# A graph kernel's prologue: edge counts shifted on TensorE, node rows gathered for 125 nodes at once, the input table split on GpSimd

## The reference, cut to what matters

```python
edge_index = jnp.stack([src, dst])
x = _layernorm(x + _L0_gnn_ref(x, src, dst, L0_gnn_W, L0_gnn_b), axis=-1)
x = _layernorm(x + _L1_gnn_ref(x, edge_weight, src, dst), axis=-1)
x = _layernorm(x + _L2_gnn_ref(x, edge_weight1, src, dst, L2_gnn_W1, L2_gnn_b1, L2_gnn_W2, L2_gnn_b2), axis=-1)
x = _layernorm(x + _L3_gnn_ref(x, edge_index, L3_gnn_W1_l, L3_gnn_b1, L3_gnn_W1_r, L3_gnn_W2_l, L3_gnn_b2, L3_gnn_W2_r), axis=-1)

# in L0, and alike in the others:
sums = jax.ops.segment_sum(h[src], dst, num_segments=N)
deg = jax.ops.segment_sum(jnp.ones((src.shape[0],), h.dtype), dst, num_segments=N)
h_total = jnp.concatenate([h, sums / jnp.maximum(deg, 1.0)[:, None]], axis=1)
```

## Time and profile before

| What | Value |
|---|---|
| median of 3 executions | 4041.06 us (4039.64 to 4046.97) |
| the profiled execution's own time | 4037.8 us |
| its span in the trace | 4035.9 us |
| busy share of the span | PE 73%, PE weight load 70%, DVE 55%, ACT 23%, POOL 35% |
| start of the first build matmul | 343.85 us |

### The profile page before, as it was taken

How to read it: one execution, slowest core, us unless ns; L and a number is a source line. 1 busy time by engine, 2 the same in 40 slices (tenths; PEclk the granted TensorE clock), 3 DMA queues, 4 the chain that set the end, 5 groups by cost and what they waited for, 6 DMA issues and landing times.

```text
span 4035.9 us, 119777 instructions
## 1 busy us (share of the span) xinstructions
PE 2965.3 (73%) x52730; PEld 2823.6 (70%) x52730; DVE 2213.4 (55%) x3076; ACT 937.2 (23%) x1994; POOL 1393.3 (35%) x1262
## 2 busy tenths in 40 slices
PE   0636999999995888888984655655555556489898
PEld 0635999999994878888874544555545555489898
DVE  8955777677766554455656555555545555411122
ACT  0004777777771000000000111111111111100000
POOL 5478100000000000000007777777777777600100
PEclk9999999999995999999996777777777777799999
DMA  4414787777884999999974333343333333287797
GB/s 122 83 35 128 272 289 286 269 284 273 287 288 163 402 403 391 403 391 404 400 325 114 93 92 99 99 109 92 91 100 97 104 97 99 69 346 288 261 380 312
DMA packets 334176, 891.87 MB, mean 221 GB/s; under 512 B 124164, under 2 KB 199032, under 8 KB 304088
## 3 DMA queue, kind: packets, MB, share of 16 engines
q1 hardware_dynamic: 279400, 835.28, 55.9%
q0 software_dynamic: 44480, 47.34, 5.6%
q10 hardware_dynamic: 9792, 1.93, 0.3%
HBM read 634.20 MB, written 250.86 MB: 219 GB/s over the span
## 4 chain that ended last, share of the span: by engine, by line
PE 32%; POOL 28%; issue 16%; DMA 15%; DVE 5%; ACT 1%; SPq 1%; POOLq 1%; DVEq 1%; ACTq 0%
POOL stream L931 27%; DMA stream<-a_weights 13%; PE ps L1287 13%; PE ps L1333 6%; PE ps L1260 5%; PE ps L1328 5%; POOL stream L909 1%; DVE junk L1615 1%; DMA a_counts<-stream 1%; ACT stream L1041 1%; DVE junk L1693 1%; DVE stream L1678 1%; PE ps L1394 1%; PE ps L1228 1%; SPq L675 0%
## 5 line engine op out<-in xcount | busy, mean ns | idle before, releaser
L931 POOL DMA_INDIRECT stream<-table,stream x990 | 1091.0, 1102 | 1998.9 <-DMA stream<-dst_run 1697.3
L1287 PE MATMUL ps<-operand_room 64*128 64x50 bf16 (+1 forms) x18750 | 635.1, 221 | 17.3 <-DVE operand_room L1860 8.0
L1475 PE MATMUL ps<-edge_room,stream 125*128 125x64 bf16 x2970 | 196.2, 242 | 609.5 <-DVE stream L2227 581.3
L1287 PEld LDWEIGHTS ps<-operand_room 64*128 64x128 bf16 x18750 | 613.8, 163 | 42.5 <-DVE operand_room L1860 8.5
L1333 PE MATMUL ps<-stream,node_room 125*64 125x125 f32 x10000 | 565.0, 273 | 92.8 <-DMA stream<-a_weights 85.6
L1475 PEld LDWEIGHTS ps<-edge_room,stream 125*128 125x128 bf16 x2970 | 185.4, 162 | 619.4 <-DVE stream L2227 416.8
L1333 PEld LDWEIGHTS ps<-stream,node_room 125*64 125x64 f32 x10000 | 542.0, 137 | 108.1 <-DMA stream<-a_weights 98.3
L1041 ACT CAST stream<-ps 128x500 bf16<-128x500 f32 (+2 forms) x700 | 431.3, 633 | 194.3 <-PE ps L1287 155.1
L1041 ACT COPY stream<-ps 128x500 f32<-128x500 f32 (+2 forms) x700 | 422.1, 619 | 0.0
L1328 PE MATMUL ps<-operand_room,stream 125*125 125x192 bf16 x3750 | 326.8, 250 | 4.4 <-POOLq L567 4.4
L1328 PEld LDWEIGHTS ps<-operand_room,stream 125*125 125x125 bf16 x3750 | 321.8, 140 | 4.6 <-POOLq L567 4.6
(11 more groups left out here) (269 smaller groups left out, 3516.4 us busy)
## 6 DMA issues: line engine op xcount, KB each, us to landing
stream<-a_weights SPq DMA_DIRECT2D x100, 3125.0 KB, 16.7
a_weights<-stream SPq DMA_DIRECT2D x500, 312.5 KB
stream<-a_counts SPq DMA_DIRECT2D x100, 1562.5 KB, 9.1
a_counts<-stream SPq DMA_DIRECT2D x500, 156.2 KB
node_room<-sorted_edges SPq DMA_DIRECT2D x120, 352.0 KB
stream<-dst_run SPq DMA_DIRECT2D x30, 1056.0 KB, 5.8
stream<-table,stream POOLq DMA_INDIRECT x990
node_room<-sorted_edges SPq DMA_DIRECT2D x40, 256.0 KB
```

Source lines behind the costliest of these rows:

```text
L931: pool.indirect_dma_start(emsg[s][:, t, :], None, tables[L2][:, :], bass.IndirectOffsetOnAxis(src_t[j % 3][:, at:at + 1], 0))\
L1287: ins = pe.matmul(out if step == 0 else out[:, 1:2], low[s][rows_a, :, t], planes[s][rows_a, t // TI, what, :, t % TI], start=step == 0, s ...
L1475: ins = pe.matmul(ps_q[:, t * D:(t + 1) * D], hot_dst[0:Q, :, at], qparts[0:Q, POOL_BLOCKS[i], v * D:(v + 1) * D], start=v == 0, stop=v == 2)
```

## The change

- `upto` gets a column of zeros on its left (`upto_pad`), and the identity matrix gets zeros around it (`ident_pad`). Two matmuls on PE, placed behind histogram 12 and a wait for `upto`, give `below`: one shifts by a partition, the other moves the last partition of a column to the first of the next. The writes to memory and the reads back are gone.
- `node_at` holds one value for each of the 125 nodes of a column. POOL gathers 125 nodes with one indirect DMA (50 in all, none of which waits for the flag), into buffers of their own.
- The 15 transposes of a chunk of keys become 30 f32 matmuls with every second column of the identity: for even nodes into partitions 0 to 63 of PSUM, for odd nodes into 64 to 127.
- The spill's table is made at column 23 of the loop instead of 32, and its 50 matmuls lie between histograms 4 to 12, six behind each (the last two behind 12).
- On DVE the wait for `below` stands behind histogram 12; 21 histograms follow it. Before, 15 stood ahead of it and 6 behind.
- The split of x is done on POOL in ten pieces of five tiles behind the gathers and the flag; PE waits for all ten ahead of block 1.

```diff
+    KG = 2
+    KGATHERS = KCH // KG
+    SPILL_FROM, SPILL_STEP, COUNTED = 4, 6, 13
...
-            sp.wait_ge(upto_rdy, 1)
-            sp.dma_start(edges_upto[1:N_NODES + 1].rearrange("(j q) -> q j", q=Q), upto[0:Q, :],
-                         allow_slow_non_contiguous=True).then_inc(upto_out, 16)
...
-            sp.wait_ge(upto_out, 48)
-            sp.dma_start(below[0:Q, :], edges_upto[0:N_NODES].rearrange("(j q) -> q j", q=Q),
-                         allow_slow_non_contiguous=True).then_inc(below_in, 16)
-            for a in range(3):
-                evens = edges_upto[a:a + N_NODES].rearrange("(j q) -> q j", q=Q)[0:Q:2, :]
-                sp.dma_start(upto3[0:COLS, a, :], evens, allow_slow_non_contiguous=True).then_inc(below_in, 16)
...
+            def gather_nodes():
+
+                for j in range(NPP):
+                    at = j % KC * DEG * 3
+                    pool.indirect_dma_start(node_rows[j // KC][0:Q, at:at + DEG * 3], None, packed[:, :],
...
                 if mode == "linear":
-                    gather_nodes(KRING, KCH)
+                    for lo in range(0, NPP, KC):
+                        split(pool, pieces(L0, lo, lo + KC), xcur[0:Q, lo:lo + KC, :], total[0][0:Q], parts_rdy)
...
-            gather_nodes(0, KRING)
+            gather_nodes()
             both(pool, run)
...
                 ins.then_inc(hist_used, 1)
-
-            pe.wait_ge(spill_rdy, 1)
-            for j in range(NPP):
-                ins = pe.matmul(bank(3)[0:Q, j:j + 1], spill[:, j, :], last_w[:, :], start=True, stop=True)
-            ins.then_inc(wspill, 1)
+                if m == SPILL_FROM:
+                    pe.wait_ge(spill_rdy, 1)
+                if m >= SPILL_FROM:
+                    for j in range((m - SPILL_FROM) * SPILL_STEP, min((m - SPILL_FROM + 1) * SPILL_STEP, NPP)):
+                        pe.matmul(bank(3)[0:Q, j:j + 1], spill[:, j, :], last_w[:, :], start=True, stop=True)\
+                          .then_inc(wspill, 1)
+                if m == COUNTED - 1:
+                    pe.wait_ge(upto_rdy, 1)
+                    pe.matmul(ps_below, ident_pad[0:Q, 0:Q], upto[0:Q, :], start=True, stop=False)
+                    pe.matmul(ps_below, ident_pad[0:Q, Q:2 * Q], upto_pad[0:Q, 0:NPP],
+                              start=False, stop=True).then_inc(below_ps, 1)
...
                         for j in range(KC):
-                            ins = pe.transpose(ps_key[c % 2][v][:, j, :], rows_of[0:PITCH, j, :, v],
-                                               ident[0:PITCH, 0:PITCH])
+                            for a in range(2):
+                                ins = pe.matmul(ps_key[c % 2][v][a * DEG:(a + 1) * DEG, j, :],
+                                                rows_of[0:Q, j, :, v], ident[0:Q, a:P:2], start=True, stop=True)
...
                 for jj in range(JI):
+                    if jj == 1:
+                        pe.wait_ge(parts_rdy, KCH)
                     build_block(0, jj)
...
-                if j == 32:
+                if j == 23:
+                    v.memset(upto_pad[:, 0:1], 0.0)
                     fill_spill(1)
...
-            for m in range(13, 28):
-                histogram(m)
-
-            v.wait_ge(below_in, 64)
+            v.wait_ge(below_ps, 1)
+            v.tensor_copy(n(below), ps_below)
+            v.drain()
+            v.tensor_copy(n(node_at), n(below)).then_inc(node_rdy, 1)
             v.tensor_tensor(n(deg), n(upto), n(below), ALU.subtract)
...
-            for m in range(28, STEPS):
+            for m in range(COUNTED, STEPS):
                 histogram(m)
...
-                    for lo, hi in ((0, PART), (PART, NPP)):
-                        split(v, pieces(L0, lo, hi), xcur[0:Q, lo:hi, :], x_rest[0:Q, lo:hi, :], parts_rdy)
                     keys()
```

More of the change, by code:

```diff
@@ L189, in build_program @@
                   .rearrange("p (u i h t) -> p u i h t", i=4, u=TO, t=TI) for b in range(2)]
[L190 to L194, removed]
+        PART = NPP // 2
+        GOTW = KC * DEG * 3
+        node_rows = [in_room(stream, c * GOTW, GOTW) for c in range(KCH - 1)] + [in_room(node_room, 0, GOTW)]
+        far_tmp = in_room(stream, KCH * GOTW, KC * DEG).rearrange("p (j t) -> p j t", t=DEG)
+        key_tmp = [in_room(stream, KCH * GOTW + (i + 1) * KC * DEG, KC * PITCH) for i in range(2)]
+        assert KG * KGATHERS == KCH and PART % KC == 0 and KC == GT and (KCH - 1) * GOTW <= 4 * CH
+        assert SPILL_FROM + -(-NPP // SPILL_STEP) <= COUNTED and GOTW <= EPP
         pack_all = in_room(operand_room, 2320, 3 * EPP).rearrange("p (t v) -> p t v", v=3)
@@ L280, in build_program @@
         start_i = sb("start_i", [P, NPP], I32)
-        node_f, blk_f, cnt, upto, below, deg, has, dinv, norm, norm_has, tmpn, wend, wcarry = (
-            sb(n, [P, NPP]) for n in ("node_f", "blk_f", "cnt", "upto", "below", "deg", "has", "dinv", "norm",
+        node_f, blk_f, cnt, below, deg, has, dinv, norm, norm_has, tmpn, wend, wcarry = (
+            sb(n, [P, NPP]) for n in ("node_f", "blk_f", "cnt", "below", "deg", "has", "dinv", "norm",
                                       "norm_has", "tmpn", "wend", "wcarry"))
-        upto3 = sb("upto3", [P, 3, NPP])
-        node_at = sb("node_at", [P, 2, NPP], I32)
-        node_deg = sb("node_deg", [P, 2, NPP])
+        node_at = sb("node_at", [P, NPP], I32)
+        upto_pad = sb("upto_pad", [P, 1 + NPP])
+        upto = upto_pad[:, 1:1 + NPP]
         first_i = sb("first_i", [P, 1], I32)
@@ L406, in build_program @@
         zero_out = sem("zero_out")
-        node_in = [sem(f"node_in{s}") for s in range(KRING)]
+        node_in = [sem(f"node_in{s}") for s in range(KGATHERS)]
         far_rdy = sem("far_rdy")
@@ L946, in run @@
                 if mode == "linear":
[L947 to L950 removed]
+                    for lo in range(0, NPP, KC):
+                        split(pool, pieces(L0, lo, lo + KC), xcur[0:Q, lo:lo + KC, :], total[0][0:Q], parts_rdy)
+                else:
+                    for i in range(KGATHERS):
+                        pool.wait_ge(node_in[i], 16 * KG * KC)
                 gather_weights()
@@ L1802, in keys @@
                 for c in range(KCH):
[L1803 to L1804 removed]
+                    if c % KG == 0:
+                        v.wait_ge(node_in[c // KG], 16 * KG * KC)
                     js = slice(c * KC, (c + 1) * KC)
[L1806 to L1811 removed]
+                    found = node_rows[c].rearrange("p (j t v) -> p j t v", j=KC, v=3)[0:Q, :, :, 0]
+                    far = far_tmp[0:Q]
+                    v.tensor_tensor(far, slot_f[0:Q, 0:DEG].unsqueeze(1).to_broadcast([Q, KC, DEG]),
+                                    deg[0:Q, js].unsqueeze(2).to_broadcast([Q, KC, DEG]), ALU.is_ge)
                     v.drain()
[L1813 to L1815 removed]
+                    v.scalar_tensor_tensor(found, far, FAR, found, ALU.mult, ALU.add)
                     v.drain()
```

55 lines of the change are left out of this document (11 added, 44 removed).

## The result

The kernel after takes **4019.86 us** in the median of 7 runs (4015.26 to 4030.09); the kernel before, run beside it, 4041.06 (4037.95 to 4049.95). The ratio is 0.9946, 95% interval 0.9932 to 0.9961: 21 us faster, where 46 were forecast. The time lies inside the range of 3984 to 4028 us, but 25 us above the forecast of 3995.

What follows compares the result with a forecast made beforehand. The chain through POOL's edge gathers and PE's build was untouched; only an earlier build start could win. Flag and split gave 31.5 us, keys 14.7: 4037.8 - 46.1 = 3991.7, median 3.3 above, so 3995 us; range 3984 to 4028.

Steps and rivals of the forecast that it cites:

- PE between the histograms: Counting loop: spill matmuls make histogram 12 start some 4 us late; after the shifts `below` is there at about 164 us.
- Flag, gathers: Prologue: flag at 219.2, keys at 220.3 instead of 251.79 us; 50 gathers all issued at 256, upper bound 272.
- A chunk of keys: Keys: 60 PE passes take 3.55 us, a chunk 7.4, ten 74; build starts at 297.7, 46.1 us earlier.
- rival 1: Keys: array halves take turns or PE runs at 1.2 GHz; chunk 10.5 us, build 15 us earlier, total 4026; chance 0.17.
- rival 3: Keys: a pass costs the spill's 0.211 us; chunk 16.7, build 47 us later, total 4088; chance 0.06.
- The split on POOL: Ten pieces beside keys and block 0 end at 296, with a stall 305, before PE needs them at 312.5 us.
- Rival 2: DVE's work stretches POOL's split to 75 us, exposing 19 to 28 us; total 4014 to 4023; chance 0.11.
- everything after it keeps its order and its waits: Behind block 0's first matmul: only that start moves, so the question is how much and whether something late holds the build.
- Rival 4: Prologue: counts come no earlier, shifts at 189, build at 323 us, total 4020; chance 0.06 together with others near no change.

## Why the prediction was wrong, point by point

- **PE between the histograms: right.** Shifts at 160.65, forecast behind some 162.9; `below` 2 us early. From the first shift to DVE's copy 1.10 us passed, forecast 1.14.
- **Flag, gathers: right.** Keys at 217.47 for 220.3. The gathers took 2.2 us each under the histograms and 1.51 after them, the last started at 252.98; I had 256 as the end.
- **A chunk of keys: right, and the deciding price.** 3.47 us for 60 passes where L1333's row gave 3.55. The first five chunks take 7.3 to 7.6 us. Rivals 1 and 3, which had a pass at 0.108 or 0.211, are out. PE's granted clock did fall, which rival 1 had named: 0.61 from 251 to 299 us, a mixture of 1.2 and 2.4 GHz, where the keys of before had 1.00. But the 60 passes took 3.47 us at either clock. Windows of after (us, busy and count of PE, PEld, DVE, ACT, POOL, then the clock): the second chunk of keys at 2.4 GHz, the ninth at 1.2, the end of the keys, and the first 24 us of the build:

```profile
226.18:229.65 3.47, 3.47 (x60) 3.28 (x60) 0.00 (x0) 0.00 (x0) 2.63 (x3) 1.00 0.25 64
280.00:285.00 5.00, 3.47 (x60) 3.32 (x60) 1.28 (x3) 0.35 (x2) 4.08 (x7) 0.50 0.01 2
251.00:299.00 48.00, 18.03 (x317) 17.06 (x314) 25.87 (x45) 4.53 (x12) 35.91 (x55) 0.61 0.04 9
299.30:323.30 24.00, 21.93 (x588) 21.30 (x589) 17.59 (x18) 19.49 (x40) 20.32 (x13) 0.72 0.32 93
```

  and the same 24 us in before:

```profile
343.85:367.85 24.00, 21.86 (x587) 21.22 (x588) 17.57 (x18) 19.41 (x40) 20.64 (x12) 0.79 0.32 92
```

  588 passes against 587: the lower clock in the keys cost the first 24 us of the build nothing. The next 24 us have 541 passes in after and 602 in before, at clocks of 0.93 and 1.00; what part of that is the clock, no run shows.
- **The split on POOL: its length right, its side effects wrong.** Ten pieces ended at 295.67 (forecast 296 to 305). Rival 2 had DVE stretch POOL, to 75 us; in after, POOL's split took 41.5 and mostly stretched DVE instead. From DVE's timeline beside the split:

```profile
277.34 0.33 DVE L1813 CAST node_room<-stream 128x320 bf16<-128x320 f32 x1
277.75 0.92 DVE L1815 TENSOR_TENSOR stream<-stream,node_room 128x320 f32<-128x320 f32 x1
278.74 0.41 DVE L1817 CAST node_room<-stream 128x320 bf16<-128x320 f32 x1
279.27 0.98 DVE L1798 TENSOR_TENSOR stream<-slot_f,deg 125x320 f32<-125x320 f32 x1
280.32 0.68 DVE L1801 SCALAR_TENSOR_TENSOR stream<-stream 125x320 f32<-125x320 f32 x1
...
285.22 0.49 DVE L1811 TENSOR_TENSOR stream<-ps,node_room 128x320 f32<-128x320 f32 x1
```

  Operations with two inputs from SBUF grow from 0.49 and 0.59 us to as much as 1.02 and 1.03; L1811, with one input from PSUM and one from SBUF, stays at 0.49. The casts L1817, with one input from SBUF, grow too, from 0.33 to as much as 0.76. The last five chunks take 7.8 to 8.5 us. That is 4 us, the difference between 299.3 and the 295.4 of the kernel with the gaps. The Trainium skill ("GPSIMD Engine Reference", section "Specifications") says that GpSimd shares its SBUF interfaces with VectorE, in contention with DVE instructions in a 2-port performance mode or with two SBUF inputs; for two inputs the trace agrees, with 0.49 against 0.98 for L1798. Whether the casts ran in such a mode no run here shows.
- **The step that failed: "everything after it keeps its order and its waits", taken to mean that everything behind the first build matmul also keeps its length.** ("From here on the change touches nothing" says the same, and is wrong for the times.) I priced the split only by when it ends, and put what POOL does later at nothing without a reason. That POOL executes the split raises the price of 990 later gathers: by 23 us in the profiled pair and 15 in the means. Added to before, it costs 23 us in the edge layer and 12 in the build that it then runs beside. Of the 23.4 us between the first build matmul's gain and the total's, some 15 are the gathers. With the split taken off POOL and put into DVE's gaps the kernel takes 3993.84 and 3996.56 us, beside the 3995 of the forecast. That it comes so close is partly luck: the first build matmul comes 2.3 us before the forecast 297.7, and the build stays 5 to 6.5 us longer than in before (877.7 and 879.3). But no other term of the sum is off by more than a few microseconds.
- **The rest of the loss, some 8 us, lies in the build.** It is 882 us in the mean of two traces of after, against 872.8 in the only trace of before on this sort of chip. The longer stall at two loop turns is shown (5.1 us instead of 2.4 at the first), and its time is 1 to 5 us. The gathers beside the build give up to 2.3. Single traces of one kernel differ by 4.5 us (884.3 and 879.8). The remainder stays open.
- **Rival 4: out.** The counts came 27.9 us earlier.

Not settled: why an executed cast makes the shortest of the later gathers 7 to 14 ns longer and their mean 16, and why L887's own minimum stays at 1205 ns with the split ahead of it. Nor why the stall depends on the loop's place; only one other place was tried.

## What to carry to other kernels

When work moves to an idle engine, its price is not only when it ends: look at what that engine does hundreds of times later, and compare the minimum duration of that one instruction between the two traces. Where the kernel's long stage waits for POOL's gathers, keep casts and additions off POOL ahead of it and look for a gap of DVE instead. Work that runs beside DVE can also stretch it, as the pieces did in the keys and, in the kernel before, in the build. Here a gap of 3.6 us lay in each of ten chunks and took the whole split. A table of stages between fixed events, before and after, finds a loss in untouched code.

## What the runs showed of the hardware

- One cast on POOL (0.3 us) ahead of 990 gathers raised their shortest from 940 to 947 ns and the kernel by 13 us; a fill did not raise the shortest, and the same cast behind them did not. A longer cast behind the node gathers raised it from 943 to 951 (one execution).
- Beside casts and subtractions of POOL, DVE's operations with two SBUF inputs grew from 0.49 to as much as 1.02 us and from 1.40 to 1.77 in the mean; one with an input from PSUM stayed at 0.49.
- Small f32 matmuls that alternate between the two halves of the array took 0.058 us a pass (3.47/60) at a granted clock of 1.00 and of 0.50 alike.
- PE's stall at the turn of a loop (209 to 214 us a turn) was 2.3 to 2.7 us with the loop at two places in its program, and 3.3 to 4.1, at some turns with 1.2 to 1.4 more behind it, at another.
- Two chips differed by 9% on the same kernel (4041 and 4395 us), and the same change was worth 21 us on one and 78 on the other, where PE stood 28.5 us in the old spill without a visible cause.
